# Nine steps of full width instead of twelve in a causal attention, and another order of TensorE's work within a step

## What is computed

```python
xn = layernorm(x)                       # over the 256 channels
q, k, v = split(xn @ W_attn + b_attn)   # 16 heads of 16 channels
q, k = rope(q), rope(k)
att = softmax(where(causal, q @ k.T / sqrt(16), -inf))
s = (att @ v) @ W_proj + b_proj
gate, up = xn @ wg.T, xn @ wu.T         # 256 -> 768, integer weights / 127
g = silu((silu(gate) * up) @ wd.T)      # 768 -> 256
out = x + s * g
```

## Time and profile before

| | us |
|---|---|
| median of three runs | 1310.66 |
| the profiled execution | 1310.76 |
| its span, from the first to the last instruction | 1309.0 |
| TensorE matmuls, busy | 1253.6 (96%) |
| VectorE busy | 1007.0 (77%) |
| ScalarE busy | 973.5 (74%) |
| GpSimd busy | 697.3 (53%) |

### The profile page before, as it was taken

The page is one execution under the profiler, slowest core; times in us unless marked ns, Lnnn a source line. Parts: engine busy times, 40 slices in busy tenths (PEclk is TensorE's granted clock), DMA queues, the critical chain, the costliest instruction groups (busy, mean ns, idle before and its releaser), DMA issues.

```text
span 1309.0 us, 30884 instructions
## 1 busy us (share of the span) xinstructions
PE 1253.6 (96%) x11580; PEld 565.5 (43%) x11580; DVE 1007.0 (77%) x1970; ACT 973.5 (74%) x2120; POOL 697.3 (53%) x859
## 2 busy tenths in 40 slices
PE   3789999999999999999999999999999999999986
PEld 2334444444344443544444443444435444444433
DVE  6678788887888878887888878888788878878712
ACT  4458777787878878787877878788787878778763
POOL 4437343674528735485436745287354854364552
PEclk9989999999999999999999999999999999999989
DMA  4130012302041030301223020410303012220101
GB/s 150 58 114 3 34 51 65 99 1 77 24 130 35 2 99 28 112 26 43 58 69 96 2 84 16 131 34 3 98 32 108 25 43 58 73 60 2 34 1 49
DMA packets 55657, 72.71 MB, mean 56 GB/s; under 512 B 8330, under 2 KB 34384, under 8 KB 55508
## 3 DMA queue, kind: packets, MB, share of 16 engines
q1 hardware_dynamic: 55496, 70.73, 17.5%
q10 hardware_dynamic: 12, 0.01, 0.0%
HBM read 44.96 MB, written 25.17 MB: 54 GB/s over the span
## 4 chain that ended last, share of the span: by engine, by line
PE 90%; ACT 5%; DVE 3%; issue 1%; POOL 1%; POOLq 0%; DVEq 0%; ACTq 0%
PE ring L820 35%; PE acc L812 21%; PE st L758 15%; PE ring L782 9%; PE ring L793 3%; PE ring L893 3%; ACT pexp L1022 2%; PE ring L929 1%; PE ring L830 1%; PE ring L908 1%; DVE mx_a L1181 1%; ACT parts L1061 1%; ACT th L1076 0%; ACT ynT L1087 0%; DVE ln L1211 0%
## 5 line engine op out<-in xcount | busy, mean ns | idle before, releaser
L1022 ACT ACTIVATE pexp<-st 128x512 f32<-128x512 f32 (+3 forms) x1536 | 662.9, 490 | 93.7 <-PE st L758 80.3
L1181 DVE TENSOR_REDUCE mx_a<-ring 128x1 f32<-128x512 f32 (+3 forms) x896 | 533.0, 644 | 84.3 <-PE ring L793 50.0
L1473 POOL TENSOR_SCALAR_AFFINE_SELECT pexp<-pexp 128x512 f32<-128x512 f32 x256 | 163.1, 637 | 451.3 <-ACT pexp L1022 444.9
L812 PE MATMUL acc<-pexp,v_pad 128*17 128x512 f32 (+3 forms) x3072 | 325.2, 496 | 4.9 <-POOL pexp L1473 4.3
L758 PE MATMUL st<-q_st,k_st 50*128 50x512 f16 (+3 forms) x1536 | 279.3, 335 | 9.8 <-ACT pexp L1022 5.7
L782 PE MATMUL ring<-k_st,q_st 48*128 48x512 f16 (+3 forms) x1536 | 250.0, 326 | 9.4 <-ACT ups L1067 3.7
L1181 DVE TENSOR_REDUCE mx_b<-ring 128x1 f32<-128x384 f32 (+3 forms) x384 | 212.2, 594 | 36.3 <-PE ring L793 33.4
L758 PEld LDWEIGHTS st<-q_st,k_st 50*128 50x128 f16 x1536 | 82.2, 93 | 361.9 <-ACT pexp L1022 253.1
L1503 POOL TENSOR_TENSOR hf<-ga,ups 128x512 f32<-128x512 f32 x96 | 122.1, 1272 | 72.3 <-issue 39.0
L793 PE MATMUL ring<-tri,ident 64*128 64x128 bf16 (+2 forms) x1536 | 114.1, 216 | 0.0
L1512 POOL TENSOR_TENSOR hT<-hf,hT 128x512 f16<-128x512 f32 x96 | 111.3, 1160 | 1.8
(11 more groups left out here) (149 smaller groups left out, 1541.2 us busy)
## 6 DMA issues: line engine op xcount, KB each, us to landing
parts_scratch<-parts SPq DMA_DIRECT2D x32, 512.0 KB, 2.8
q_st<-parts_scratch SPq DMA_DIRECT2D x186, 64.0 KB, 2.2
k_st<-parts_scratch SPq DMA_DIRECT2D x186, 64.0 KB, 2.2
xo<-in_x SPq DMA_DIRECT2D x32, 256.0 KB, 3.2
out<-xo SPq DMA_DIRECT2D x32, 256.0 KB, 2.2
xn<-in_x SPq DMA_DIRECT2D x7, 1024.0 KB, 6.0
q_st<-mT SPq DMA_DIRECT2D x126, 4.0 KB
xn<-in_x SPq DMA_DIRECT2D x2, 512.0 KB, 6.1
```

What stands on the lines that cost most here:

```text
L812: mm = nc.tensor.matmul(acc[32 * j:32 * j + D + 1, CH - w:CH], v_pad[:, kb, GH * g + j, :], pexp[:, GH * (n % NSET) + j, 0:w], start=n in ...
L1022: nc.scalar.activation(pexp[:, GH * (n % NSET) + j, 0:w], st[:, (GH * n + j) % NST, 0:w], ACT.Exp, scale=1.0 / (QK_SCALE * np.sqrt(D))).th ...
L1181: nc.vector.reduce_max(dst, ring[:, b, 0:len(heads) * w].rearrange("p (s w) -> p s w", w=w), AX.X)\
L1473: nc.gpsimd.affine_select(out=t, in_=t, compare_op=ALU.is_ge, fill=0.0, base=0, pattern=[[0, GH], [1, P]], channel_multiplier=-1).then_inc ...
```

## The change

The twelve blocks of a unit are packed into nine steps, each exactly 512 queries wide for each head: three steps hold two blocks each (384 and 128, or 256 and 256 wide). A step's exponentials are four instructions of 512 columns; its scores and values are still one matmul for each block and head, so both keep their numbers. One step (`MIXED`) holds a block of either half of the queries; the values of its second block are made with those of the step after it. The maxima are packed likewise into 18 parts of 512 columns, two in each slot: kind F is one whole row of keys, E is 512 wide with the diagonal, A is a pair of 384 and 128, B two heads of 256. VectorE reduces each part of a different query block by itself. The eight masks of a unit now fall into steps 0, 1, 2, 6 and 7, with two each in steps 1, 2 and 7.

A batch has 36 slots, and the maxima run 12 slots ahead. TensorE's order in a slot is now: maxima, part 0; scores, first half; tasks; values of the step before; scores, second half; maxima, part 1. ScalarE copies `acc` before the step's first exponentials instead of behind them. The table of tasks is new: one slot of 36 has no TensorE task, where three of 48 had none.

```diff
-STEPS = 12
+STEPS = 9
+MIXED = 2
-LEAD = 16
+LEAD = 12
-BLOCKS = [(0, 0), (0, 2), (0, 3), (0, 1), (1, 0), (1, 1), (1, 6), (1, 2), (1, 4), (1, 7), (1, 5), (1, 3)]
+BLOCKS = [[(0, 0)], [(0, 1), (0, 3)], [(0, 2), (1, 6)], [(1, 0)], [(1, 1)], [(1, 2)], [(1, 4)], [(1, 5), (1, 7)], [(1, 3)]]
+ITEMS = ('AF', 'BF', 'EF', 'BF', 'EF', 'AE', 'EF', 'AF', 'AF')
...
+            found[n, half] = {"A": [(4 * c + 2, c * CH, 3 * P, p), (4 * c, c * CH, P, p)],
+                              "B": [(4 * c + 1, c * CH, 2 * P, k) for k in range(2)],
+                              "E": [(4 * c + 3, c * CH, 4 * P, p)],
+                              "F": [(c, 0, CH, p)]}[kind]
...
 TASKS = {
+    0: [("DN", 1, 2), ("FT", 0)],
+    1: [("XC", 0), ("DN", 1, 3)],
+    2: [("UPU", 0, 0), ("UPG", 0, 0), ("YT", 3, 1)],
+    3: [("UPG", 0, 1), ("V", 0, 1), ("FP", 0)],
+    4: [("UPU", 0, 1), ("LNS", 0), ("FT", 1)],
+    5: [("FP", 1)],
+    6: [("LNS", 1), ("UPU", 0, 2), ("UPG", 0, 2)],
+    7: [("LNS", 2), ("MT", 1), ("UPG", 0, 3), ("LNS", 3)],
+    8: [("V", 1, 1), ("V", 1, 0)],
+    9: [("LNR",)],
...
+    14: [("UPG", 1, 0)],
...
+    19: [("QK", 0, 0, 1), ("TX", 1, 0), ("TX", 0, 0), ("DN", 0, 1)],
+    20: [("QK", 0, 0, 0), ("QK", 0, 1, 0), ("DN", 0, 2)],
+    21: [("DN", 0, 3)],
...
             def scores(i, g, n, p):
...
+                for qc, kb, at in placed(n):
...
+                    for a in range(2):
+                        index = GH * (STEPS * (4 * i + g) + n) + 2 * p + a
+                        if at == 0:
+
+                            wait(pe, exp_done, index - NST + 1)
...
             def values(i, g, n):
...
+                found = value_blocks(n)
+                for k, (m, block_) in enumerate(found):
...
+                                              start=k == 0 and n in (0, MIXED + 1),
+                                              stop=k == len(found) - 1 and n in (MIXED, STEPS - 1))
                 mm.then_inc(pv_done, 1)
...
-                    for half in range(2):
-                        scores(i, g, n, half)
-                        for m in maxima_at(kind, slot, half):
-                            maxima(kind, i, m[1], m[2])
-                        if half == 0:
-                            for t in tasks_at(kind, slot):
-                                task(kind, i, t)
-                        elif slot > 0:
-                            values(i, *divmod(slot - 1, STEPS))
-                        elif kind != "first":
-                            values(i - 1, GROUPS - 1, STEPS - 1)
+                    for m in maxima_at(kind, slot, 0):
+                        maxima(kind, i, m[1], m[2])
+                    scores(i, g, n, 0)
+                    for t in tasks_at(kind, slot):
+                        task(kind, i, t)
+                    if slot > 0:
+                        values(i, *divmod(slot - 1, STEPS))
+                    elif kind != "first":
+                        values(i - 1, GROUPS - 1, STEPS - 1)
+                    scores(i, g, n, 1)
+                    for m in maxima_at(kind, slot, 1):
+                        maxima(kind, i, m[1], m[2])
...
                 if p == 0:
-                    wait(act, pv_done, step - NSET + 1)
+                    wait(act, pv_done, step - NSET + 1 + (n == MIXED + NSET))
...
+                    for t, k0, w, heads in parts_of_bank:
...
+                        top_ = nc.vector.reduce_max(dst, src, AX.X)
+                        at += len(heads) * w
+                    top_.then_inc(ring_free[b], 1)
...
+                for at in diagonals(n):
+                    t = pexp[:, GH * (n % NSET):GH * (n % NSET) + GH, at:at + P]
+                    nc.gpsimd.affine_select(out=t, in_=t, compare_op=ALU.is_ge, fill=0.0, base=0,
+                                            pattern=[[0, GH], [1, P]], channel_multiplier=-1).then_inc(tri_done, 1)
```

More of the change, by code:

```diff
@@ new lines, in placed, with diagonals, value_blocks, item_segments @@
+def placed(n):
+    found, at = [], 0
+    for qc, kb in BLOCKS[n]:
+        found.append((qc, kb, at))
+        at += width(qc, kb)
+    assert at == CH
+    return found
+def diagonals(n):
+    return [at for qc, kb, at in placed(n) if kb >= 4 * qc]
+def value_blocks(n):
+    return [(n, k) for k in range(len(BLOCKS[n])) if (n, k) != (MIXED, 1)] + [(MIXED, 1)] * (n == MIXED + 1)
+def item_segments():
+    rest = {k: [(c, p) for c in range(2) for p in range(2)] for k in "AE"}
+    rest["B"] = [(c, None) for c in range(2)]
+    rest["F"] = [(t, p) for t in range(4, TT) for p in range(2)]
+    found = {}
+    for n, kinds in enumerate(ITEMS):
+        for half, kind in enumerate(kinds):
+            c, p = rest[kind].pop(0)
+            found[n, half] = {"A": [(4 * c + 2, c * CH, 3 * P, p), (4 * c, c * CH, P, p)],
+                              "B": [(4 * c + 1, c * CH, 2 * P, k) for k in range(2)],
+                              "E": [(4 * c + 3, c * CH, 4 * P, p)],
+                              "F": [(c, 0, CH, p)]}[kind]
+    assert not any(rest.values())
+    return found
@@ L321, in ln_number, with diag_count @@
     return 0 if kind == "pro" else i + 1
-def diag_count(N_unit, n):
-    return 2 * GH * N_unit + sum(is_diag(m) for m in range(n + 1))
+def diag_count(unit, n):
+    each = [len(diagonals(m)) for m in range(STEPS)]
+    return unit * sum(each) + sum(each[:n + 1])
 def wait(eng, sem, count):
@@ L719, in body @@
                                 load_xo(i - 1, 1)
-                        if half == 0 and slot == 3:
+                        if half == 0 and slot == 2:
                             load_stacks(i, 3, 2 * i + 2)
@@ L781, in maxima @@
                         rows = slice(SIDE * a, SIDE * a + MROW)
-                        mm = nc.tensor.matmul(dst[:, k * w:(k + 1) * w], q_st[rows, g, p, t * P:(t + 1) * P],
-                                              k_st[rows, g, p, k0:k0 + w], start=k == 0, stop=half == 1)
-                        if half == 1:
+                        mm = nc.tensor.matmul(dst[:, at:at + w], q_st[rows, g, p, t * P:(t + 1) * P],
+                                              k_st[rows, g, p, k0:k0 + w], start=k == 0, stop=not diag[0])
+                        if not diag[0]:
                             mm.then_inc(ready, 1)
-                if half == 0:
-                    n = len(heads)
+                    at += w
+                if diag[0]:
+                    n = len(found)
+                    pitch = found[-1][2]
                     for h in range(2):
@@ L792, in maxima @@
                             rows = slice(SIDE * a, SIDE * a + 64)
-                            mm = nc.tensor.matmul(ring[:, b, 0:n * w].rearrange("p (s w) -> p s w", s=n)[:, :, w - keys:w],
-                                                  ident64[rows, h, :], tri[rows, 0:n, 0:keys], start=False, stop=h == 1)
+                            tail = ring[:, b, CH - n * pitch:CH].rearrange("p (s w) -> p s w", s=n)[:, :, pitch - keys:pitch]
+                            mm = nc.tensor.matmul(tail, ident64[rows, h, :], tri[rows, 0:n, 0:keys], start=False, stop=h == 1)
                             if h == 1:
```

221 lines of the change are left out of this document (88 added, 133 removed).

## The result

The kernel with the change takes 1321.32 us (median of five runs, 1318.06 to 1322.6), the one before 1310.66 (five, 1308.68 to 1311.75): a ratio of 1.0075 [1.0058, 1.0093], slower by 0.75%. The forecast was 1312, its own range 1298 to 1328. The profiled execution took 1321.38 us.

A forecast was written before the change was run, and what follows sets the result against it. TensorE, busy 96% of the span, was taken as the bound. A middle batch summed -8.4 - 2.7 + 8.9 + 1.8 + 0.8 = +0.4 us; with the other batches +1 on 1310.8 gave 1312 us, range 1298 to 1328.

The forecast's parts named there:

- (a): TensorE between kinds of array use: fewer changes a slot, task to values taken at 0.12 us; -8.4 us a batch.
- (e): GpSimd's masks have less time before the values, which wait in a few slots: +0.8 us a batch.
- the rival that this step is free: Faster rival: TensorE's task to values costs nothing, -4.2 us a batch; 0.27, shared with VectorE and GpSimd staying on time.
- (b): TensorE's remaining time over columns and changes of use, read as waits of the old order that go: -2.7 us a batch.
- (c): First half's second score head waits for the third exponential of the step before, until 1.08 us: +8.9 us a batch.
- the ring: First task's bank waits for VectorE's first reduction: priced +1.8 us a batch; as slower rival 1334 or 1355, chance 0.13.
- (d): VectorE's 44 reductions a unit for 40: 1.6 us a batch more work; first task's bank just fits; lateness +1.8.
- The forecast's own sign for the ring: TensorE waiting for VectorE in front of most slots' first task would show that the four-bank ring decides.
- (f): ScalarE: 1152 exponentials instead of 1536, 39 us less busy, off the path.
- (g): DMA of the next batch's first stacks: 12.6 us between store and use, before 16; no wait taken.
- The first batch ... -0.6: First batch: fewer tasks, and empty slots there cost 2.5 us; -0.6 us in all.
- by slots I get -1: Last batch: its last third has no maxima, but the same exponential wait stood there before; -1 us.

The follow-up runs named there:

- Experiments 4 to 6: Changed kernel with half the columns left out of each step's third exponential, of part 1's first reduction, or of both: 1317.64, 1311.13, 1267.22 us.
- experiment 7: Changed kernel with TensorE's order maxima part 0, scores first half, tasks, scores second half, maxima part 1, values: 1290.69 us, 0.9856 of the kernel before.
- experiment 1: Changed kernel, nine packed steps kept, with TensorE's order in a slot put back to that of the kernel before: 1293.04 us, 0.9869 of the kernel before.
- experiment 10: Kernel of experiment 7 with one of the last batch's two last projections a slot earlier: 1295.46 us, 0.9869 of the kernel before.

## Why the prediction came out as it did

*What bounds.* Right: TensorE is 91% of the chain, and what moved the middle batches was inside its busy time.

*(a) Fewer changes of use, -8.4.* The price of the step that no row showed, task to values, is 0.11 to 0.14 us in 100 of the 175 places of five batches, the least is 0.10, and in most of the others a wait comes on top; 0.12 had been taken. In sum with its waits it is 5.5 us a batch, forecast 4.2 and the 0.8 of (e). So the rival that this step is free fell. The Trainium skill, TensorEngine Tiling (Array Packing), Key Properties, says that a change of tiling mode drains TensorE. This trace agrees: all 175 places cost.

*(b) and (c), waits that go and the one that comes.* The chain of (c) came out to the hundredth: 1.08 us in the slots. So did the sum: TensorE's starts, less the columns (126.3 us a batch), leave 26.4 us a batch before and 26.2 after. Of these, 15.3 stand from rows work to task, 5.5 from task to values, 4.8 from values to scores and 0.55 in the slot without a task; less 12.5 for changes of use and 2.8 for starts within groups, 10.9 are waits, forecast 8.9 + 1.8 + 0.8 = 11.5. The forecast of a middle batch was +0.4, measured -0.2. That the 2.7 us of the old order's waits go, as (b) has it, no run shows by itself.

*But the parts are not separate terms.* The prediction priced the exponential at 8.9 and the ring at 1.8, as if one could go without the other. Experiments 4 to 6 show them in one place: 0.2 and 1.1 alone, 6.6 together. The "just fits" of (d) was right as a statement on the first task's bank, and wrong as a cost: the reduction is no wait on top, it is the floor under the other one. The forecast's own sign for the ring, that TensorE waits for VectorE in front of most slots' first task, is there: in 125 of the 175 places the load of that task waits for a reduction. But the cost tied to it, 0.15 us a slot on top, is not. That the sum came out so close, with a split of the terms that was wrong, is in part luck.

*(d) VectorE's 10 us more.* Wrong: its busy time is 1007.4, before 1007.0, and the reductions' own 530.6 + 210.6 = 741.2, before 745.2:

```profile
L1181 DVE TENSOR_REDUCE mx_a<-ring 128x1 f32<-128x512 f32 (+3 forms) x896 | 533.0, 644 | 84.3 <-PE ring L793 50.0 <-PE ring L782 26.9
...
L1181 DVE TENSOR_REDUCE mx_b<-ring 128x1 f32<-128x384 f32 (+3 forms) x384 | 212.2, 594 | 36.3 <-PE ring L793 33.4
```

The narrow ones were there before, two heads of 128 in one instruction; now each stands behind one of 384 and overlaps with its tail. Two banks of 384 and 128 take 1.41 us in the trace, two of 512 take 1.29, so a split costs 0.06 and not 0.1.

*(e) GpSimd, (f) ScalarE, (g) DMA.* The waits of values for masks are 21.5 us, before 20.5. ScalarE fell by 44 us, forecast 39, off the path as stated. No transfer comes late in a middle batch.

*The sum's ends: the step that failed.* "The first batch ... -0.6" was +4.4, and "by slots I get -1" for the last was +7.5. By slots one sees neither the clock nor the ring's debt: the last batch lost to the clock, the first to waits. The prediction had seen 0.96 in the last window and priced all slots at 2.4 GHz. A third of the last batch has no maxima to put beside ScalarE's chain; TensorE was busy for three quarters of the 8 us ahead of the fall, then the clock stood at its lower level for twice as long as before, and for 17 us at the end where it had been 3.4. By the count above the clock makes 6.3 of the 7.5. Why the clock fell for so long in this kernel stays open: before, and in experiment 7, it was as idle for 8 to 12 us with a short fall or none. The sum also counts six middle batches beside the second, the first and the last; there are five, which is worth 0.4 us.

*The test set beforehand.* "Under 150 or over 157 refutes": 152.51. 1321 lies within the forecast's own range, and on the side that had been given 0.48.

## What to carry to other kernels

A slot's order decides which latencies have cover: taking a long, independent piece of work (here the values) from between two halves that feed another engine turns that engine's latency into time of the bounding one, and it can cost more than the changes of mode that it saves (28 us here, experiment 1 to the kernel after). Before pricing a wait, ask what else is due at that same point; two waits that end together are worth next to nothing one by one, and only an experiment that takes away both shows their sum. Price first and last iterations by themselves, from their own windows and granted clock: a change that ties in the steady state was decided there.

## What the runs showed of the hardware

- The two halves of the array by rows run apart: in the kernel after, one head's scores start 0.12 to 0.33 us behind the other's in each slot of a middle batch, and the pair then lasts up to 0.71 us where 0.39 is one's own.
- Of the changes of use, values to rows is the dearest and the steadiest: 0.131 to 0.138 us in all of the 180 places of five batches of the kernel after.
- The same kernel took 1288 or 1297 us on the same chip, at a mean clock of 0.994 or 0.983 (experiment 10). In its profiled execution, one of the longer ones, the clock fell at 1240.3. Up to that point its last batch is that of experiment 7: the products start at the same times to 0.01 us, all 1.04 to 1.05 us later, and in experiment 7 the clock did not fall there. The windows, experiment 10 and then the same place in experiment 7:

```profile
1230.00:1240.00 10.00, 9.16 (x60) 2.88 (x56) 2.18 (x5) 8.42 (x16) 4.96 (x7) 1.00 0.00 1
1240.00:1250.00 10.00, 9.37 (x62) 2.85 (x63) 0.42 (x1) 5.99 (x13) 5.20 (x7) 0.66 0.01 3
```
```profile
1229.00:1239.00 10.00, 9.13 (x60) 2.88 (x56) 2.15 (x5) 8.46 (x16) 4.95 (x7) 1.00 0.00 1
```

After 110 us of the same work at the same times the clock fell in one execution and not in the other. So the kernel's work ahead of that point does not by itself decide it; what does stays open. A difference of some us between two kernels with such an end wants several runs and their mean clocks.
